# Expert stage of a routed transformer layer: the activated row is turned by VectorE in 32 by 32 blocks instead of by TensorE

## The chip, the cores and the metric

The kernel runs on one core of a Trainium2 chip. The metric is the device time of one execution in microseconds (us), the median of several runs. Every time of an instruction comes from one profiled execution.

## The reference, cut to what matters

The whole kernel computes an attention-like sampling layer, then a transformer block with multi-head attention and a mixture of experts, each followed by a layer norm. The change touches only the last part, the experts:

```python
logits = xf @ gate_w + gate_b
one_hot = jax.nn.one_hot(jnp.argmax(logits, axis=-1), E)
h = gelu(jnp.einsum('td,edh->teh', xf, w1), approximate=True)   # d = 256, h = 1024, E = 8
y = jnp.einsum('teh,ehd->ted', h, w2)
out = jnp.einsum('te,ted->td', one_hot, y)
...
x = _layernorm(x + L0_ffn(x), axis=-1)
```

There are 4096 tokens of 256 channels, in float32. Each token goes to one expert.

## The kernel before, in words

`build` runs its stages one after the other: wave parameters and sampling, gate and projection, attention, `project_and_route`, and last `experts` (L1742). The router has sorted the tokens by expert into a scratch tensor in memory, `routed`, in tiles of 128 tokens. No tile mixes experts, which makes MT = 39 tiles (L30). Two small tables, `tile_row` (named `at` in the code) and `expert`, say for each tile where its rows start and which expert it belongs to. The weights of all experts, `w1` and `w2`, lie in SBUF by then.

`experts` has one program for each engine, and semaphores order them. For tile j:

- SyncE (`load`, L1776) reads the row number from the table and loads the normalised row `z` (one buffer) and the residual row `res` (ring of 8).
- TensorE (`turn`, L1863) transposes z into PSUM `pZ`, and ScalarE (`norm`, L1815) applies the norm's weight and bias while it copies that to `zT`.
- TensorE's up projection (L1880) multiplies zT by w1 of the expert into `pH` (128 tokens by 1024 hidden values, two banks of PSUM). ScalarE's GELU (L1825) writes `hs` (`ex_h` in the profile), tokens on partitions.
- The down projection needs hidden values on partitions. So TensorE transposes the eight 128 by 128 squares of hs into PSUM `pT` (L1897), and VectorE copies all of pT to `hT` (L1853).
- TensorE's down projection (L1891) accumulates eight products of hT with w2 into `pY`, one expert row of 256 channels.
- VectorE adds the residual (L1842), takes mean and variance (L1844, L1848, with a one-element copy L1847 between them that makes the second wait for the first), and normalises (L1856), after GpSimd has computed 1/sqrt(variance + eps) (L1800, L1802). GpSimd then sends the row to its token's place in the output with an indirect DMA (L1805).

Order of work: each engine's program is written by hand, one tile deep. In iteration j TensorE does up(j), turn(j+1), down(j-1) and the transposes of hs(j). All tiles but the first and last two run in a hardware loop (`skewed`, L1761, with `Fori`). GpSimd's program is written out for all 39 tiles. `z`, `zT`, `hs`, `hT`, `pZ`, `pH`, `pT` and `pY` all have one buffer.

Of the kernel before, what the change touches and what calls it, by code (L numbers as in the profile page):

```python
# [18 lines left out]
KC = C // P  # L19
# [9 lines left out]
E, HID = 8, 1024  # L29
MT = TILES + E - 1  # L30
REGION = TOKENS + P
ROW = 2 * C + 4
# [22 lines left out]
def build(nc, io, dr):  # L55

    with ExitStack() as top:
# [39 lines left out]
        with ExitStack() as ctx:  # L97
            experts(nc, sem, lambda *a: sb(ctx, *a), lambda *a: ps(ctx, *a), io, dr, ident, w1, w2, expert, at)
# [1643 lines left out]
def experts(nc, sem, sb, ps, io, dr, ident, w1, w2, expert, at):  # L1742


    HC = HID // P
    ln_w, ln_b = sb("ex_lnw", [P, KC]), sb("ex_lnb", [P, KC])
    RES, OUTS = 8, 4
    z = sb("ex_z", [P, C])
    res = sb("ex_res", [P, RES, ROW - C])
    x, xo, st, mv, seen = sb("ex_x", [P, C]), sb("ex_out", [P, OUTS, C]), sb("ex_st", [P, 6]), sb("ex_mv", [P, 2]), sb("ex_seen", [P, 1])  # L1750
    eps, power, ve, rs = (sb("ex_" + n, [P, 1]) for n in ("eps", "power", "ve", "rs"))
    zT = sb("ex_zT", [P, KC, P])
    hs, hT = sb("ex_h", [P, HID]), sb("ex_hT", [P, HC, P])
    pZ, pH, pT, pY = ps("ex_pZ", [P, KC, P]), ps("ex_pH", [P, HID]), ps("ex_pT", [P, HC, P]), ps("ex_pY", [P, C])
    w_in, z_in, turned, zd, up, gelu, hturned, hTd, down, added = (sem("ex_" + n) for n in (
        "w_in", "z_in", "turned", "zT", "up", "gelu", "h_turned", "hT", "down", "added"))
    res_in, consts, stats, waited, aggred, inv, outd = (sem("ex_" + n) for n in ("res_in", "consts", "stats", "waited", "aggr", "rstd", "out"))
    sent = [sem(f"ex_sent{i}") for i in range(2)]
    out = io["out"].rearrange("b l c -> (b l) c")

    def skewed(eng, tile):  # L1761

        tile(0, None, True)
        tile(1, 0, True)
        with eng.Fori(2, MT - 1) as j:
            tile(j, j - 1, True)
        tile(MT - 1, MT - 2, False)
        tile(None, MT - 1, False)

    with nc.Block() as block, nc.allow_non_contiguous_dma(reason="per-channel vectors"):  # L1770
        @block.sync
        def _(sp):
            sp.dma_start(ln_w[:], io["L0_ffn_ln2_w"].rearrange("(k p) -> p k", p=P)).then_inc(w_in, 16)
            sp.dma_start(ln_b[:], io["L0_ffn_ln2_b"].rearrange("(k p) -> p k", p=P)).then_inc(w_in, 16)  # L1774

            def load(j):  # L1776
                row = sp.value_load(at[0:1, bass.ds(j, 1)], min_val=0, max_val=E * REGION - P)  # L1777
                if not isinstance(j, int) or j:

                    sp.wait_ge(turned, j)  # L1780
                sp.dma_start(z[:], dr["routed"][bass.ds(row, P), 0:C]).then_inc(z_in, 16)
                sp.dma_start(res[:, bass.ds(j % RES, 1), :].rearrange("p o c -> p (o c)"), dr["routed"][bass.ds(row, P), C:ROW]).then_inc(res_in, 16)

            load(0)
            with sp.Fori(1, MT) as j:
                load(j)

        @block.gpsimd
# [22 lines left out]
        @block.scalar  # L1811
        def _(a):
            a.wait_ge(w_in, 32)

            def norm(j):  # L1815
                a.wait_ge(turned, j + 1)
                a.wait_ge(up, j)
                for k in range(KC):
                    a.activation(zT[:, k, :], pZ[:, k, :], ACT.Identity, bias=ln_b[:, k:k + 1], scale=ln_w[:, k:k + 1]).then_inc(zd, 1)  # L1819

            def tile(j, prev, more):
                if j is not None:
                    a.wait_ge(up, j + 1)
                    a.wait_ge(hturned, j)
                    a.activation(hs[:], pH[:], ACT.Gelu_apprx_tanh).then_inc(gelu, 1)  # L1825
                if more:
                    norm(j + 1)

            norm(0)
            skewed(a, tile)  # L1830

        @block.vector
        def _(dve):
            v = nc.vector

            def tile(j, prev, more):
                if prev is not None:
                    dve.wait_ge(down, prev + 1)
                    dve.wait_ge(res_in, prev * 16 + 16)
                    if not isinstance(prev, int) or prev:  # L1840
                        dve.wait_ge(outd, prev)
                    v.tensor_tensor(x[:], pY[:], res[:, bass.ds(prev % RES, 1), 0:C].rearrange("p o c -> p (o c)"), ALU.add).then_inc(added, 1)  # L1842
                    dve.wait_ge(added, prev + 1)
                    v.bn_stats(st[:], x[:]).then_inc(stats, 1)  # L1844
                    dve.wait_ge(stats, prev + 1)

                    v.tensor_copy(seen[:], st[:, 0:1]).then_inc(waited, 1)  # L1847
                    v.bn_aggr(mv[:], st[:]).then_inc(aggred, 1)  # L1848
                if j is not None:
                    dve.wait_ge(hturned, j + 1)  # L1850
                    if prev is not None:
                        dve.wait_ge(down, j)
                    v.tensor_copy(hT[:], pT[:]).then_inc(hTd, 1)  # L1853
                if prev is not None:
                    dve.wait_ge(inv, prev * 2 + 2)
                    v.tensor_scalar(xo[:, bass.ds(prev % OUTS, 1), :].rearrange("p o c -> p (o c)"), x[:], mv[:, 0:1], rs[:],  # L1856
                                    ALU.subtract, ALU.mult).then_inc(outd, 1)

            skewed(dve, tile)

        @block.tensor
        def _(pe):
            def turn(j):  # L1863
                pe.wait_ge(z_in, j * 16 + 16)
                pe.wait_ge(zd, j * KC)
                for k in range(KC):
                    last = nc.tensor.transpose(pZ[:, k, :], z[:, k * P:(k + 1) * P], ident[:])  # L1867
                last.then_inc(turned, 1)

            def which(j):  # L1870
                return pe.value_load(expert[0:1, bass.ds(j, 1)], min_val=0, max_val=E - 1)

            def tile(j, prev, more):
                if j is not None:
                    e = which(j)
                    pe.wait_ge(zd, j * KC + KC)
                    pe.wait_ge(gelu, j)
                    for n in range(HID // 512):
                        for k in range(KC):
                            last = nc.tensor.matmul(pH[:, n * 512:(n + 1) * 512], zT[:, k, :],  # L1880
                                                    w1[:, k, bass.ds(e, 1), n * 512:(n + 1) * 512], start=(k == 0), stop=(k == KC - 1))
                    last.then_inc(up, 1)
                if more:
                    turn(j + 1)
                if prev is not None:
                    e = which(prev)
                    pe.wait_ge(hTd, prev + 1)
                    if j is None or not isinstance(j, int) or prev:
                        pe.wait_ge(added, prev)
                    for c in range(HC):  # L1890
                        last = nc.tensor.matmul(pY[:], hT[:, c, :], w2[:, c, bass.ds(e, 1), :], start=(c == 0), stop=(c == HC - 1))  # L1891
                    last.then_inc(down, 1)
                if j is not None:
                    pe.wait_ge(gelu, j + 1)
                    pe.wait_ge(hTd, j)
                    for c in range(HC):
                        last = nc.tensor.transpose(pT[:, c, :], hs[:, c * P:(c + 1) * P], ident[:])  # L1897
                    last.then_inc(hturned, 1)

            turn(0)  # L1900
            skewed(pe, tile)


SCRATCH = {
# [33 lines left out]
```

## Time and profile before

| what | value |
|---|---|
| median of 3 runs | 1881.21 us (1880.91 to 1882.89) |
| time of the profiled execution | 1883.31 us |
| its span, first to last instruction | 1881.1 us |
| expert stage, first SyncE instruction to the end of the span | 1550.09 to 1881.1 us |
| TensorE (PE) busy over the span | 86% |
| VectorE (DVE) busy over the span | 68% |

Engine names in rows: PE is TensorE's matrix unit, PEld its weight load, DVE VectorE, ACT ScalarE, POOL GpSimd, SP SyncE. Busy time counts an engine's running instructions; two that overlap in its pipeline count once in a stretch, so the mean duration of one instruction and the distance from one start to the next (the pitch below) can differ. Times are from the start of the span.

### The profile page before, as it was taken

The numbers are of one execution on the slowest core, as the hardware profiler recorded it, in microseconds if no ns is written. First come the engines' busy times: TensorE is split into PE (matmuls) and PEld (weight loads), VectorE is DVE, ScalarE is ACT, GpSimd is POOL, SyncE is SP. The second block draws the span as 40 slices with busy tenths as digits, with TensorE's granted clock in tenths as the row PEclk, the third lists the DMA queues.
The fourth block names the chain that finished last, engine by engine and source line by source line (L and its number), as shares of the span: only waits on it lengthen the run. The fifth ranks groups of instructions, "written<-read, shape, count | busy, mean of one in ns | idle before, by whom it ended". The sixth has DMA issues, their size and how long they took to land. (4 is left out here: it accounts for less than half of the span.)

```text
span 1881.1 us, 33148 instructions
## 1 busy us (share of the span) xinstructions
PE 1622.6 (86%) x9382; PEld 806.5 (43%) x9383; DVE 1273.7 (68%) x2358; ACT 1003.4 (53%) x1696; POOL 255.9 (14%) x426
## 2 busy tenths in 40 slices
PE   5049788878996899999999999999996829999997
PEld 5036555544553122322332332323225725777765
DVE  4889798754553888889888888888844742333333
ACT  3178797843444277767676777777772212222221
POOL 0011111102333000000000000000002661222222
PEclk9579999988998699999999999999998759999999
DMA  3010110113655532222222222223213531111110
GB/s 95 0 52 18 38 35 18 37 52 102 216 195 180 90 74 70 72 67 71 70 68 70 73 74 73 73 73 73 52 29 107 168 135 46 47 50 50 50 50 15
DMA packets 156230, 137.89 MB, mean 73 GB/s; under 512 B 73774, under 2 KB 129775, under 8 KB 156144
## 3 DMA queue, kind: packets, MB, share of 16 engines
q1 hardware_dynamic: 150096, 121.92, 23.5%
q0 software_dynamic: 5072, 14.77, 2.1%
q8 instruction: 31, 0.51, 0.1%
q14 instruction: 55, 0.45, 0.1%
q10 hardware_dynamic: 976, 0.24, 0.1%
HBM read 88.16 MB, written 49.23 MB: 73 GB/s over the span
## 5 line engine op out<-in xcount | busy, mean ns | idle before, releaser
L1253 DVE TENSOR_REDUCE at_mx<-at_pmx 128x1 f32<-128x512 f32 x1024 | 648.3, 682 | 75.8 <-PE at_pmx L1325 75.0
L1240 ACT ACTIVATE at_p<-at_pst 128x512 f32<-128x512 f32 x1024 | 540.0, 601 | 251.6 <-PE at_pst L1344 243.1
L1325 PE MATMUL at_pmx<-at_k,at_q 96*128 96x512 bf16 x1024 | 400.6, 393 | 16.9 <-DMA at_k<-scratch_ks 16.2
L1344 PE MATMUL at_pst<-at_q,at_k 99*128 99x512 bf16 x1024 | 352.2, 381 | 12.4 <-ACT at_p L1240 10.0
L1354 PE MATMUL at_pacc<-at_p,at_v 128*32 128x512 f32 x2048 | 272.7, 604 | 0.9 <-ACT at_p L1240 0.7
L1325 PEld LDWEIGHTS at_pmx<-at_k,at_q 96*128 96x128 bf16 x1024 | 99.7, 97 | 270.9 <-DVE at_mx L1253 196.2
L527 ACT ACTIVATE ws_A<-ws_steps,par_beta,par_alpha 128x672 f32<-128x672 bf16 (+2 forms) x256 | 200.4, 854 | 21.5 <-DVE ws_steps L603 16.0
L616 DVE TENSOR_TENSOR ws_AT<-ws_pA,ws_hitT 128x768 f32<-128x768 f32 (+1 forms) x192 | 180.5, 952 | 41.5 <-PE ws_pA L675 40.2
L675 PE MATMUL ws_pA<-ident,ws_A 128*128 128x128 f32 x1088 | 150.6, 285 | 26.0 <-ACT ws_A L527 21.2
L1344 PEld LDWEIGHTS at_pst<-at_q,at_k 99*128 99x128 bf16 x1024 | 99.3, 98 | 161.6 <-ACT at_p L1240 98.4
L1825 ACT ACTIVATE ex_h<-ex_pH 128x1024 f32<-128x1024 f32 x39 | 39.9, 1023 | 239.9 <-PE ex_pH L1880 239.9
L675 PEld LDWEIGHTS ws_pA<-ident,ws_A 128*128 128x128 f32 x1088 | 121.4, 145 | 84.8 <-DVE ws_AT L616 53.4
L1842 DVE TENSOR_TENSOR ex_x<-ex_pY,ex_res 128x256 f32<-128x256 f32 x39 | 16.5, 424 | 203.3 <-PE ex_pY L1891 203.3
L1880 PE MATMUL ex_pH<-w,ex_zT 128*128 x312 | 142.1, 599 | 1.0 <-ACT ex_zT L1819 1.0
L1891 PE MATMUL ex_pY<-w,ex_hT 128*128 x624 | 141.2, 379 | 1.6 <-DVE ex_hT L1853 1.6
L1891 PEld LDWEIGHTS ex_pY<-w,ex_hT 128*128 128x128 f32 x624 | 115.6, 190 | 16.4 <-issue 2.3
L1491 POOL MEMSET pg_eps<- 128x4 f32 x1 | 0.1, 106 | 803.5 <-POOLq L1121 803.5
L1880 PEld LDWEIGHTS ex_pH<-w,ex_zT 128*128 128x128 f32 x312 | 56.9, 192 | 58.4 <-issue 58.4
L1354 PEld LDWEIGHTS at_pacc<-at_p,at_v 128*32 128x32 f32 x2048 | 40.9, 107 | 94.4 <-ACT at_p L1240 61.5
L695 PE MATMUL ws_acc<-ws_AT,ws_x 128*32 128x384 f32 (+3 forms) x768 | 77.4, 480 | 0.0
L673 PE MATMUL ws_pA<-identb,ws_hit 128*128 128x128 bf16 x136 | 10.5, 232 | 73.9 <-DVE ws_steps L603 73.8
L1853 DVE COPY ex_hT<-ex_pT 128x1024 f32<-128x1024 f32 x39 | 47.7, 1223 | 27.7 <-PE ex_pT L1897 27.7
(237 smaller groups left out, 1659.1 us busy)
## 6 DMA issues: line engine op xcount, KB each, us to landing
w<-in_L_ffn_w SPq DMA_DIRECT2D x32, 512.0 KB, 4.8
at_q<-scratch_qs SPq DMA_DIRECT2D x192, 64.0 KB, 2.9
at_k<-scratch_ks SPq DMA_DIRECT2D x192, 64.0 KB, 3.0
scratch_v<-gp_v SPq DMA_DIRECT2D x8, 1024.0 KB, 5.6
at_v<-scratch_v SPq DMA_DIRECT2D x32, 256.0 KB, 3.5
scratch_qs<-gp_split SPq DMA_DIRECT2D x16, 384.0 KB, 2.6
scratch_ks<-gp_split SPq DMA_DIRECT2D x16, 384.0 KB, 3.4
ex_res<-scratch_routed SPq DMA_DIRECT2D x39, 130.0 KB, 2.3
```

The source lines that it names most:

```text
L527: nc.scalar.activation(A[:, h % QUAD, cols(g, r)], KB[g][:, cols(g, r)], ACT.Exp, bias=par["beta"][:, t, h], scale=par["alpha"][:, t, h]). ...
L616: v.tensor_tensor(AT[h // QUAD][:, home(h, m[0]):home(h, m[-1]) + 1, :].rearrange("p s l -> p (s l)"), p[:, 0:len(m) * P], mask, ALU.mult) ...
L675: last = nc.tensor.transpose(p[:, to], a, ident[:])
L695: last = nc.tensor.matmul(acc[hq][h4 * WD:(h4 + 1) * WD, rs[0] * P:(rs[-1] + 1) * P], xb[:, j, h * WD:(h + 1) * WD], AT[hq][:, home(h, s): ...
L1240: a.activation(pt[k // 2 % 4][:, k % 2, :], pst[bank(k)][:], ACT.Exp).then_inc(exped, 1)
L1253: v.reduce_max(mx[u % 2][:, m // 2, m % 2:m % 2 + 1], pmx[bank(m)][:], AX.X).then_inc(red, 1)
L1325: nc.tensor.matmul(pmx[bank(m)][:], qst[u][0:ROWS, h, nt * P:(nt + 1) * P], kst[u][0:ROWS, h, kh * HALF:(kh + 1) * HALF], start=True, stop ...
L1344: nc.tensor.matmul(pst[bank(k)][:], kst[u][:, h, t * P:(t + 1) * P], qst[u][:, h, p * HALF:(p + 1) * HALF], start=True, stop=True).then_in ...
L1354: last = nc.tensor.matmul(pacc[at:at + 2 * DK, :], vst[u][:, s, h, :], pt[(2 * s + p) % 4][:, h, :], start=(s == 0), stop=(s == BT - 1))
L1853: v.tensor_copy(hT[:], pT[:]).then_inc(hTd, 1)
L1880: last = nc.tensor.matmul(pH[:, n * 512:(n + 1) * 512], zT[:, k, :], w1[:, k, bass.ds(e, 1), n * 512:(n + 1) * 512], start=(k == 0), stop= ...
L1891: last = nc.tensor.matmul(pY[:], hT[:, c, :], w2[:, c, bass.ds(e, 1), :], start=(c == 0), stop=(c == HC - 1))
```

## The change

TensorE's eight transposes of hs and the PSUM tile pT go away, with VectorE's copy of 128 by 1024. In their place VectorE issues 16 transposes a tile. One takes 32 partitions of hs (quarter q), and of each of the eight 128-column squares the 32 columns of block b. It turns the eight 32 by 32 blocks so taken and writes them to the 32 partitions of quarter b of hT, in columns q*32 to q*32+32 of each square. So one such instruction has 256 elements on each of 32 partitions, source and destination in SBUF, both float32, and each of the 16 pairs (q, b) has one. VectorE's order for iteration j is: transposes with q = 0 and 1 of tile j, addition and statistics of tile j-2, transposes with q = 2 and 3 of tile j, normalisation of tile j-2. Nothing waits between the eight transposes of a half.

z, zT, hs, hT, pZ and pY get two buffers. pH keeps one. TensorE's iteration is up(j), turn(j+1), down(j-2). The loop over tiles is written out for all engines. SyncE loads tile 0's z ahead of the norm's weight and bias, and its loads wait for `turned` of one tile earlier than before. GpSimd's program is unchanged.

```diff
-    zT = sb("ex_zT", [P, KC, P])
-    hs, hT = sb("ex_h", [P, HID]), sb("ex_hT", [P, HC, P])
-    pZ, pH, pT, pY = ps("ex_pZ", [P, KC, P]), ps("ex_pH", [P, HID]), ps("ex_pT", [P, HC, P]), ps("ex_pY", [P, C])
+    zT = [sb(f"ex_zT{i}", [P, KC, P]) for i in range(2)]
+    hs, hT = ([sb(f"ex_{n}{i}", [P, HC, P]) for i in range(2)] for n in ("h", "hT"))
+    pZ = [ps(f"ex_pZ{i}", [P, KC, 2 * P]) for i in range(2)]
+    pH, pY = ps("ex_pH", [P, HID]), [ps(f"ex_pY{i}", [P, 2 * C]) for i in range(2)]
...
+            def load(j):
+                row = sp.value_load(at[0:1, j:j + 1], min_val=0, max_val=E * REGION - P)
+                if j >= 2:
+
+                    sp.wait_ge(turned, j - 1)
+                    sp.wait_ge(res_in[j % 2], j // 2 * 16)
+                sp.dma_start(z[j % 2][:], dr["routed"][bass.ds(row, P), 0:C]).then_inc(z_in[j % 2], 16)
+                if j >= RES:
+                    sp.wait_ge(sent[j % 2], (j - RES) // 2 * 16 + 16)
+                sp.dma_start(res[:, j % RES, :], dr["routed"][bass.ds(row, P), C:ROW]).then_inc(res_in[j % 2], 16)
+
...
+            norm(0)
+            for j in range(MT):
+                a.wait_ge(up, j + 1)
+                if j >= 2:
+                    a.wait_ge(hTd, j - 1)
+                a.activation(hs[j % 2][:].rearrange("p c n -> p (c n)"), pH[:], ACT.Gelu_apprx_tanh).then_inc(gelu, 1)
+                if j + 1 < MT:
                     norm(j + 1)
-
-            norm(0)
-            skewed(a, tile)
 
...
-                    v.tensor_copy(hT[:], pT[:]).then_inc(hTd, 1)
...
+            def turn_h(j, lanes):
+
+                u = j % 2
+                if 0 in lanes:
+                    dve.wait_ge(gelu, j + 1)
+                    if j >= 2:
+                        dve.wait_ge(down, j - 1)
+                for q in lanes:
+                    for b in range(P // Q):
+                        last = v.transpose(hT[u][b * Q:(b + 1) * Q, :, q * Q:(q + 1) * Q], hs[u][q * Q:(q + 1) * Q, :, b * Q:(b + 1) * Q])
+                if P // Q - 1 in lanes:
+                    last.then_inc(hTd, 1)
+
+            def add(j):
+                dve.wait_ge(down, j + 1)
+                dve.wait_ge(res_in[j % 2], j // 2 * 16 + 16)
+                if j:
+                    dve.wait_ge(outd, j)
+                v.tensor_tensor(x[:], pY[j % 2][:, 0:C], res[:, j % RES, 0:C], ALU.add).then_inc(added, 1)
+                dve.wait_ge(added, j + 1)
+                v.bn_stats(st[:], x[:]).then_inc(stats, 1)
+                dve.wait_ge(stats, j + 1)
+
+                v.tensor_copy(seen[:], st[:, 0:1]).then_inc(waited, 1)
+                if j:
+                    dve.wait_ge(inv, j * 2)
+                v.bn_aggr(mv[:], st[:]).then_inc(aggred, 1)
+
...
+            for j in range(MT + 2):
+                if j < MT:
+                    turn_h(j, range(0, 2))
+                if j >= 2:
+                    add(j - 2)
+                if j < MT:
+                    turn_h(j, range(2, 4))
+                if j >= 2:
+                    normalise(j - 2)
 
...
+            for j in range(MT + 2):
+                if j < MT:
                     e = which(j)
                     pe.wait_ge(zd, j * KC + KC)
-                    pe.wait_ge(gelu, j)
+                    if j:
+                        pe.wait_ge(gelu, j)
...
+                if j + 1 < MT:
                     turn(j + 1)
-                if prev is not None:
-                    e = which(prev)
-                    pe.wait_ge(hTd, prev + 1)
-                    if j is None or not isinstance(j, int) or prev:
-                        pe.wait_ge(added, prev)
+                if j >= 2:
+                    e = which(j - 2)
+                    pe.wait_ge(hTd, j - 1)
+                    if j >= 4:
+                        pe.wait_ge(added, j - 3)
                     for c in range(HC):
-                        last = nc.tensor.matmul(pY[:], hT[:, c, :], w2[:, c, bass.ds(e, 1), :], start=(c == 0), stop=(c == HC - 1))
+                        last = nc.tensor.matmul(pY[j % 2][:, 0:C], hT[j % 2][:, c, :], w2[:, c, bass.ds(e, 1), :], start=(c == 0), stop=(c == HC - 1))
                     last.then_inc(down, 1)
-                if j is not None:
-                    pe.wait_ge(gelu, j + 1)
-                    pe.wait_ge(hTd, j)
-                    for c in range(HC):
-                        last = nc.tensor.transpose(pT[:, c, :], hs[:, c * P:(c + 1) * P], ident[:])
```

## Rows read from the trace of the kernel before

**Rows 1.** Busy time in one stretch of the stage; columns as in the header.

```profile
core 0: us, PE busy (x) PEld busy (x) DVE busy (x) ACT busy (x) POOL busy (x), PEclk, DMA share, GB/s
1625.00:1665.00 40.00, 40.00 (x172) 27.85 (x172) 13.29 (x30) 8.60 (x15) 8.87 (x15) 1.00 0.16 49
```

**Rows 2.** Chain of waits, one period: start us, us, what.

```profile
1643.32 3.44 PE ex_pH L1880 x8
1646.76 0.22 PE ex_pZ L1867 x2
1646.98 3.46 PE ex_pY L1891 x16
1650.43 0.87 PE ex_pT L1897 x8
1651.31 3.44 PE ex_pH L1880 x8
```

**Rows 3.** Groups by line in the expert stage: busy us, mean ns | idle before, releaser.

```profile
L1853 DVE COPY ex_hT<-ex_pT 128x1024 f32<-128x1024 f32 x39 | 47.7, 1223 | 27.7 <-PE ex_pT L1897 27.7
...
L1825 ACT ACTIVATE ex_h<-ex_pH 128x1024 f32<-128x1024 f32 x39 | 39.9, 1023 | 239.9 <-PE ex_pH L1880 239.9
...
L1842 DVE TENSOR_TENSOR ex_x<-ex_pY,ex_res 128x256 f32<-128x256 f32 x39 | 16.5, 424 | 203.3 <-PE ex_pY L1891 203.3
```

**Rows 4.** Timeline of VectorE, one tile: start us, us.

```profile
1650.81 0.42 DVE L1842 TENSOR_TENSOR ex_x<-ex_pY,ex_res 128x256 f32<-128x256 f32 x1 [5.24 <-PE ex_pY L1891]
1651.27 0.43 DVE L1844 BATCH_NORM_STATS2 ex_st<-ex_x 128x6 f32<-128x256 f32 x1
1651.73 0.15 DVE L1847 COPY ex_seen<-ex_st 128x1 f32<-128x1 f32 x1
1651.81 0.17 DVE L1848 BATCH_NORM_AGGREGATE ex_mv<-ex_st 128x2 f32<-128x6 f32 x1
1651.90 1.22 DVE L1853 COPY ex_hT<-ex_pT 128x1024 f32<-128x1024 f32 x1
1653.14 0.41 DVE L1856 TENSOR_SCALAR ex_out<-ex_x,ex_mv,ex_rs 128x256 f32 x1
```

**Rows 5.** Timeline of VectorE in the routing stage, four operations without a wait.

```profile
1509.54 1.41 DVE L1622 BATCH_NORM_STATS2 pg_st<-pg_x 128x6 f32<-128x256 f32 x4
```

**Rows 6.** Groups of VectorE by shape, whole span.

```profile
L1622 DVE BATCH_NORM_STATS2 pg_st<-pg_x 128x6 f32<-128x256 f32 x32 | 11.2, 414 | 0.3
...
L1667 DVE TENSOR_TENSOR pg_past<-pg_js,pg_cum 1x312 f32<-1x312 f32 x1 | 0.5, 472 | 0.0
```

**Rows 7.** Chain of waits, start and end of the stage.

```profile
1550.09 0.38 SPq L1773
1550.52 0.46 SPq L1774
...
1561.27 1.03 ACT ex_h L1825
1562.35 1.09 PE ex_pT L1897 x8
...
1868.08 0.13 issue
1868.21 2.01 PE ex_pY L1891 x9
```

**Rows 8.** Timeline of the last tile, with the idle time before it.

```profile
1868.21 3.72 PE L1891 MATMUL ex_pY<-w,ex_hT 128*128 x16 [1.58 <-DVE ex_hT L1853]
...
1875.36 1.03 POOL L1805 DMA_INDIRECT out<-ex_out,ex_res  x1 [1.26 <-DVE ex_out L1856]
```

**Rows 9.** Timeline of the routing stage: VectorE beside GpSimd.

```profile
1513.39 3.42 DVE L1633 TENSOR_SCALAR pg_n<-pg_x,pg_mv,pg_rs 128x256 f32<-128x256 f32 x4 [1.98 <-POOL pg_rs L1525]
1513.95 2.39 POOL L1530 TENSOR_TENSOR pg_rows<-pg_x,pg_y 128x1024 f32<-128x1024 f32 x1 [0.59 <-DMA scratch_routed<-pg_rows,pg_slot]
```

**Rows 10.** Busy time and granted clock in three stretches.

```profile
1554.00:1559.00 5.00, 3.77 (x6) 1.81 (x7) 0.00 (x0) 2.09 (x3) 0.00 (x0) 0.50 0.23 63
...
1515.00:1530.00 15.00, 6.59 (x52) 5.96 (x52) 7.39 (x34) 2.38 (x3) 10.07 (x14) 0.50 0.37 142
1868.20:1871.90 3.70, 3.69 (x16) 2.96 (x16) 0.19 (x1) 0.00 (x0) 1.02 (x1) 1.00 0.01 0
```

More of the change, by code:

```diff
@@ L1745, in experts @@
     HC = HID // P
+    Q = 32
     ln_w, ln_b = sb("ex_lnw", [P, KC]), sb("ex_lnb", [P, KC])
     RES, OUTS = 8, 4
-    z = sb("ex_z", [P, C])
+    z = [sb(f"ex_z{i}", [P, C]) for i in range(2)]
     res = sb("ex_res", [P, RES, ROW - C])
@@ L1751, in experts @@
     eps, power, ve, rs = (sb("ex_" + n, [P, 1]) for n in ("eps", "power", "ve", "rs"))
-    zT = sb("ex_zT", [P, KC, P])
-    hs, hT = sb("ex_h", [P, HID]), sb("ex_hT", [P, HC, P])
-    pZ, pH, pT, pY = ps("ex_pZ", [P, KC, P]), ps("ex_pH", [P, HID]), ps("ex_pT", [P, HC, P]), ps("ex_pY", [P, C])
-    w_in, z_in, turned, zd, up, gelu, hturned, hTd, down, added = (sem("ex_" + n) for n in (
-        "w_in", "z_in", "turned", "zT", "up", "gelu", "h_turned", "hT", "down", "added"))
-    res_in, consts, stats, waited, aggred, inv, outd = (sem("ex_" + n) for n in ("res_in", "consts", "stats", "waited", "aggr", "rstd", "out"))
+    zT = [sb(f"ex_zT{i}", [P, KC, P]) for i in range(2)]
+    hs, hT = ([sb(f"ex_{n}{i}", [P, HC, P]) for i in range(2)] for n in ("h", "hT"))
+    pZ = [ps(f"ex_pZ{i}", [P, KC, 2 * P]) for i in range(2)]
+    pH, pY = ps("ex_pH", [P, HID]), [ps(f"ex_pY{i}", [P, 2 * C]) for i in range(2)]
+    w_in, turned, zd, up, gelu, hTd, down, added = (sem("ex_" + n) for n in (
+        "w_in", "turned", "zT", "up", "gelu", "hT", "down", "added"))
+    z_in = [sem(f"ex_z_in{i}") for i in range(2)]
+    res_in = [sem(f"ex_res_in{i}") for i in range(2)]
+    consts, stats, waited, aggred, inv, outd = (sem("ex_" + n) for n in ("consts", "stats", "waited", "aggr", "rstd", "out"))
     sent = [sem(f"ex_sent{i}") for i in range(2)]
     out = io["out"].rearrange("b l c -> (b l) c")
[L1761 to L1768, printed above, removed]
     with nc.Block() as block, nc.allow_non_contiguous_dma(reason="per-channel vectors"):
@@ L1772, in _ @@
         def _(sp):
+            def load(j):
[7 more added lines that the diff above has]
+                sp.dma_start(res[:, j % RES, :], dr["routed"][bass.ds(row, P), C:ROW]).then_inc(res_in[j % 2], 16)
+            load(0)
             sp.dma_start(ln_w[:], io["L0_ffn_ln2_w"].rearrange("(k p) -> p k", p=P)).then_inc(w_in, 16)
             sp.dma_start(ln_b[:], io["L0_ffn_ln2_b"].rearrange("(k p) -> p k", p=P)).then_inc(w_in, 16)
[L1776 to L1785, printed above, removed]
+            for j in range(1, MT):
                 load(j)
@@ L1816, in norm @@
                 a.wait_ge(turned, j + 1)
-                a.wait_ge(up, j)
+                if j >= 2:
+                    a.wait_ge(up, j - 1)
                 for k in range(KC):
-                    a.activation(zT[:, k, :], pZ[:, k, :], ACT.Identity, bias=ln_b[:, k:k + 1], scale=ln_w[:, k:k + 1]).then_inc(zd, 1)
-            def tile(j, prev, more):
-                if j is not None:
[L1823 to L1826, printed above, removed]
+                    a.activation(zT[j % 2][:, k, :], pZ[j % 2][:, k, 0:P], ACT.Identity, bias=ln_b[:, k:k + 1],
+                                 scale=ln_w[:, k:k + 1]).then_inc(zd, 1)
+            norm(0)
[5 more added lines that the diff above has]
+                if j + 1 < MT:
                     norm(j + 1)
-            norm(0)
-            skewed(a, tile)
         @block.vector
@@ L1834, in _ @@
             v = nc.vector
-            def tile(j, prev, more):
-                if prev is not None:
[L1838 to L1852, printed above, removed]
-                    v.tensor_copy(hT[:], pT[:]).then_inc(hTd, 1)
[L1854 to L1857, printed above, removed]
@@ L1859, in _ @@
-            skewed(dve, tile)
+            def turn_h(j, lanes):
[9 more added lines that the diff above has]
+                    last.then_inc(hTd, 1)
@@ new lines, in normalise @@
+            def normalise(j):
+                dve.wait_ge(inv, j * 2 + 2)
+                if j >= OUTS:
+                    dve.wait_ge(sent[j % 2], (j - OUTS) // 2 * 16 + 16)
+                v.tensor_scalar(xo[:, j % OUTS, :], x[:], mv[:, 0:1], rs[:], ALU.subtract, ALU.mult).then_inc(outd, 1)
+            for j in range(MT + 2):
[7 more added lines that the diff above has]
+                    normalise(j - 2)
@@ L1863, in turn @@
             def turn(j):
-                pe.wait_ge(z_in, j * 16 + 16)
-                pe.wait_ge(zd, j * KC)
+                pe.wait_ge(z_in[j % 2], j // 2 * 16 + 16)
+                if j >= 2:
+                    pe.wait_ge(zd, (j - 1) * KC)
                 for k in range(KC):
-                    last = nc.tensor.transpose(pZ[:, k, :], z[:, k * P:(k + 1) * P], ident[:])
+                    last = nc.tensor.transpose(pZ[j % 2][:, k, 0:P], z[j % 2][:, k * P:(k + 1) * P], ident[:])
                 last.then_inc(turned, 1)
@@ L1870, in which @@
             def which(j):
-                return pe.value_load(expert[0:1, bass.ds(j, 1)], min_val=0, max_val=E - 1)
-            def tile(j, prev, more):
-                if j is not None:
+                return pe.value_load(expert[0:1, j:j + 1], min_val=0, max_val=E - 1)
+            turn(0)
+            for j in range(MT + 2):
+                if j < MT:
                     e = which(j)
                     pe.wait_ge(zd, j * KC + KC)
-                    pe.wait_ge(gelu, j)
+                    if j:
+                        pe.wait_ge(gelu, j)
@@ L1878, in tile @@
                     for n in range(HID // 512):
                         for k in range(KC):
-                            last = nc.tensor.matmul(pH[:, n * 512:(n + 1) * 512], zT[:, k, :],
+                            last = nc.tensor.matmul(pH[:, n * 512:(n + 1) * 512], zT[j % 2][:, k, :],
                                                     w1[:, k, bass.ds(e, 1), n * 512:(n + 1) * 512], start=(k == 0), stop=(k == KC - 1))
                     last.then_inc(up, 1)
-                if more:
+                if j + 1 < MT:
@@ L1884, in tile @@
                     turn(j + 1)
-                if prev is not None:
-                    e = which(prev)
-                    pe.wait_ge(hTd, prev + 1)
-                    if j is None or not isinstance(j, int) or prev:
-                        pe.wait_ge(added, prev)
+                if j >= 2:
+                    e = which(j - 2)
+                    pe.wait_ge(hTd, j - 1)
+                    if j >= 4:
+                        pe.wait_ge(added, j - 3)
                     for c in range(HC):
-                        last = nc.tensor.matmul(pY[:], hT[:, c, :], w2[:, c, bass.ds(e, 1), :], start=(c == 0), stop=(c == HC - 1))
+                        last = nc.tensor.matmul(pY[j % 2][:, 0:C], hT[j % 2][:, c, :], w2[:, c, bass.ds(e, 1), :], start=(c == 0), stop=(c == HC - 1))
@@ L1892, in tile @@
                     last.then_inc(down, 1)
-                if j is not None:
-                    pe.wait_ge(gelu, j + 1)
-                    pe.wait_ge(hTd, j)
-                    for c in range(HC):
-                        last = nc.tensor.transpose(pT[:, c, :], hs[:, c * P:(c + 1) * P], ident[:])
-                    last.then_inc(hturned, 1)
-            turn(0)
-            skewed(pe, tile)
 SCRATCH = {
```

## The prediction

> **What bounds the kernel now.** I read the stage by windows first: between 1625 and 1665 us TensorE is busy for all of 40.00 us at a granted clock of 1.00, and VectorE for 13.29 us [rows 1]. So TensorE sets the pace here, and VectorE is two thirds idle. The chain of waits says the same in detail: one tile is up projection 3.44, turning z 0.22, down projection 3.46, turning the activated row 0.87 us, 7.99 in all, one behind the other with no wait between [rows 2]. The other engines wait for TensorE: in the groups by line VectorE's addition stands behind 203.3 us of idle time that TensorE ended, ScalarE's GELU behind 239.9 us [rows 3]. The sum of the four parts is the period, so the hardware loop costs nothing now and writing it out can give nothing.
>
> **The part that goes.** TensorE loses 0.87 us a tile, which lies wholly on the path [rows 2]: 39 x 0.87 = 34 us is the most that the change can bring. TensorE's tile becomes 3.44 + 0.22 + 3.46 = 7.12 us. VectorE loses the copy of 128 by 1024, 1.22 us [rows 4], which was beside TensorE's work and is worth nothing by itself.
>
> **The part that comes.** VectorE gets 16 transpositions a tile, of 256 elements in each of 32 partitions. That only 32 partitions take part doesn't make one cheap: an operation on a single partition with 312 elements took 472 ns, one on 128 partitions with 256 elements 414 ns [rows 6]. What counts is the number of elements a partition, and so the 16 cost 16 operations of 256 elements. No row shows a transposition on VectorE. The pitch from one to the next is bounded by two patterns. Four operations of 128 by 256 with no wait between, all on the same partitions, took 1.41 us together [rows 5] at 0.41 each [rows 6]: (1.41 - 0.41) / 3 = 0.33 us pitch, since each begins while the one before is still running. Where one waits for the other's result, the pitch is 0.46 us: 1650.81 to 1651.27, and again to 1651.73 [rows 4].
>
> I take 0.46. Each of the 16 writes another quarter of the partitions than the one before, and the overlap was only seen where nothing moves, so I count none. Around it: with no overlap and no gap either it would be the duration alone, 0.42. Upwards, a block of 32 columns must be in before its first turned column can come out. By rows 4 an element costs (1.22 - 0.42) / 768 = 1.04 ns, so filling costs 33 ns, and emptying as much again: 0.46 + 0.067 = 0.53.
>
> A rule of the Trainium skill speaks against this change as well: the page "VectorE: DVE Perf Modes", section "Two Vector instructions with no wait between them", says that an instruction whose input or output starts in another group of 32 partitions than that of the last one starts only when every earlier one has finished. All 16 would be held by it. No trace here shows it, since all operations of VectorE before start at partition 0. By the rule the pitch is a full duration; without it the time would be that of the first rival.
>
> VectorE's other work for a tile: from the addition's start to the end of the statistics 1650.81 to 1651.98, 1.17 us; the normalisation 0.41 and a gap of 0.04 [rows 4]. Together 1.62. VectorE's tile is then 16 x 0.46 + 1.62 = **8.98 us, against TensorE's 7.12**. VectorE becomes the bound, and TensorE waits 1.9 us a tile for hT.
>
> **The sum.** VectorE starts on tile 0 when its GELU is done, at 1562.35 [rows 7]. From then it runs without a break: 39 x 7.36 = 287.0 for transpositions, 37 x 1.62 = 59.9 for the tiles finished between them, less 0.45 because the last normalisation stands behind the last transposition. With 0.13 us from hT to TensorE [rows 7] the last down projection starts at 1562.35 + 287.0 + 59.9 - 0.45 + 0.13 = 1909.0, where it was 1868.21 [rows 7, 8]. What follows it stays the same: 3.72 us of products, addition, statistics, normalisation, the last transfer [rows 8]. That is +40.8 us on a span of 1881.1: 1921.9, or 1924.1 for the profiled execution's 1883.3. The median shown is 2.1 us below that execution, so I forecast **1922 us**.
>
> **Edits with no price, and what covers them.** The waits added to VectorE's path: ahead of the first transposition of tile j it waits for down(j-2), which TensorE can start as soon as tile j-2 is turned, nearly a whole period earlier, and which takes 3.46 of 8.98 us. The wait for GpSimd's root (1651.98 to 1653.14, 1.16 us [rows 4]) now has eight transpositions in front, 3.7 us. ScalarE's GELU(j) now waits until tile j-2 is turned, with norm(j+1) queued behind it and so up(j+1). It is released 0.45 us before VectorE takes up tile j-1, and its 1.02 us [rows 3] are needed one tile later. With a period of 7.12 these covers would still hold: a down projection ends 3.66 us before the next one begins. z's load is one tile earlier, with a second buffer; it didn't stand in the chain of the steady tiles. SyncE issues z ahead of two small loads of 0.38 and 0.46 us [rows 7], worth 0.8 us at most once, and nothing where ScalarE then waits for those two; I take nothing.
>
> **Price of being wrong on the pitch.** 624 transpositions make 6.24 us for each 0.01 us. The change breaks even where 40.8 us are saved: 0.46 - 0.065 = 0.395 us.
>
> **Rivals.**
> First, on the other side: the 16 overlap like those of rows 5. Pitch 0.33, VectorE 16 x 0.333 + 1.62 = 6.95 us a tile, below 7.12. TensorE stays the bound. It does up(1) and turn(2) until 1566.0, then 37 tiles of 7.12 until 1829.5; VectorE turns tile 38 with an addition and statistics in between (5.33 + 1.17, + 0.13), and the last down projection starts at 1836.1: -32.1, **1849 us**. For it: no semaphore stands between the 16 and none reads what another writes, as in rows 5. Against it: they change partitions at each step. It decides at a pitch below 0.395. Chance 0.13.
>
> Second, VectorE is blocked by GpSimd. In the routing stage four operations from SBUF to SBUF took 3.42 us beside a GpSimd operation of 2.39 us, where 1.41 is the undisturbed time [rows 5, 9]. GpSimd is busy for 8.87 us in 40, 1.77 a tile [rows 1]. If all of it blocked transpositions: 37 x 1.77 = +65, 1987 us. Against it: addition, statistics and normalisation run clear of GpSimd now, and only one of the kinds of operation, the normalising one, shows the effect. Beside it stands a transposition that moves an element in two steps: pitch 0.46 + 0.27 = 0.73, +168, 2090 us. Also TensorE's clock: it was 0.50, its lower level of 1.2 GHz, where TensorE had stood idle for long before or was busy for 6.59 of 15 us, but 1.00 after a wait of 1.58 us before the last down projection [rows 8, 10]. Here it is busy for 7.12 of 8.98 with pauses of 1.9 us; I count on 1.00, and the slack of 1.9 us would take up part of a fall. Together 0.06.
>
> Third, the pitch comes out within 0.006 of 0.395, and gain and loss cancel: 1881 us. Chance 0.01.
>
> **Numbers.** The forecast, VectorE the bound at a pitch of 0.41 to 0.53, has 0.80. Its ends are 1922 - 31 = 1891 and 1922 + 42 = 1964 us, and as it holds 8 in 10 alone, the range is its own: 1890 to 1964. Faster by over 0.2% (about what a measurement of this kernel can tell from no change) is the first rival, 0.13; within 0.2% 0.02, the third rival and the edge of the forecast beside it; slower the rest, 0.85.
>
> **What would show it.** Right: VectorE busy for nearly all of each tile; period 8.6 to 9.9 us; the last of its waits before TensorE's down projection, about 1.9 us a tile; starts of the transpositions one full duration apart, and the 4 within the same input quarter no closer than those across two; ScalarE and GpSimd as before. Wrong: TensorE still busy throughout and a period of 7.12 (first rival); transpositions longer where GpSimd is at work, or one with a duration of over 0.6 us (second); a granted clock below 1.00 in the steady tiles.

## The result and the profile after

The changed kernel takes **1912.87 us** (median of 4 runs, 1912.18 to 1917.05), the kernel before beside it 1881.86 us (4 runs). The ratio is 1.0169, 95% interval 1.0157 to 1.0182: slower by 1.7%, 31 us. The profiled execution took 1912.18 us, with a span of 1910.5 us. Forecast were 1922 us and a range of 1890 to 1964.

The page of the changed kernel: span, busy time of TensorE, and the chain that ended last by engine and by line (L1842 is the new transposition).

```profile
span 1910.5 us, 32366 instructions
PE 1599.3 (84%) x9070; PEld 775.1 (41%) x9070; DVE 1497.4 (78%) x2943; ACT 1003.3 (53%) x1696; POOL 256.5 (13%) x426
...
DVE 15%; issue 3%; PE 1%; POOL 0%; DMA 0%; SPq 0%; ACT 0%; POOLq 0%
DVE ex_hT L1842 12%; DVE ex_st L1853 1%; DVE ex_x L1851 1%; DVE ex_out L1865 1%; PE ex_pH L1899 0%; DVE ex_seen L1856 0%; PE ex_pY L1910 0%; DVE ex_mv L1859 0%; DMA ex_lnb<-in_L_ffn_ln_b 0%; POOL out L1802 0%; ACT ex_h L1825 0%; ACT ex_zT L1817 0%; SPq L1769 0%; POOL ex_rs L1799 0%; SPq L1780 0%
```

Of the whole span 15% is now VectorE's chain in this stage. In the kernel before the same line of the page had TensorE there:

```profile
PE 17%; issue 0%; DVE 0%; DMA 0%; POOL 0%; SPq 0%; ACT 0%; POOLq 0%; ACTq 0%
```

Busy time in a stretch of the stage, with the header of the columns, answers to [rows 1]:

```profile
core 0: us, PE busy (x) PEld busy (x) DVE busy (x) ACT busy (x) POOL busy (x), PEclk, DMA share, GB/s
1660.00:1700.00 40.00, 33.17 (x122) 22.24 (x122) 38.49 (x96) 8.60 (x15) 8.12 (x13) 1.00 0.18 50
```

VectorE is busy for 38.5 of 40 us (before 13.3), and TensorE only for 33.2 of 40 (before 40.0). TensorE's clock stayed at 1.00 through its short pauses. The groups by line answer to [rows 3]:

```profile
L1842 DVE STREAM_TRANSPOSE ex_hT<-ex_h 32x256 f32<-32x256 f32 x624 | 271.8, 436 | 37.0 <-ACT ex_h L1825 28.2
...
L1802 POOL DMA_INDIRECT out<-ex_out,ex_res x39 | 40.1, 1027 | 147.3 <-DVE ex_out L1865 143.1 <-issue 4.2
L1825 ACT ACTIVATE ex_h<-ex_pH 128x1024 f32<-128x1024 f32 x39 | 39.9, 1023 | 260.8 <-DVE ex_hT L1842 237.0 <-PE ex_pH L1899 23.8
...
L1851 DVE TENSOR_TENSOR ex_x<-ex_pY,ex_res 128x256 f32<-128x256 f32 x39 | 16.6, 425 | 0.9 <-PE ex_pY L1910 0.3
```

The 624 transpositions take 436 ns each. The waits have turned round: the addition, which stood behind 203.3 us of TensorE's work, now waits for 0.9 us in all, and GELU's idle time is ended by VectorE (237.0 us) and only for 23.8 us by TensorE. The timeline of VectorE for one tile answers to [rows 4] (start us, us):

```profile
1700.20 0.42 DVE L1851 TENSOR_TENSOR ex_x<-ex_pY,ex_res 128x256 f32<-128x256 f32 x1
1700.66 0.43 DVE L1853 BATCH_NORM_STATS2 ex_st<-ex_x 128x6 f32<-128x256 f32 x1
1701.12 0.15 DVE L1856 COPY ex_seen<-ex_st 128x1 f32<-128x1 f32 x1
1701.19 0.17 DVE L1859 BATCH_NORM_AGGREGATE ex_mv<-ex_st 128x2 f32<-128x6 f32 x1
1701.39 3.59 DVE L1842 STREAM_TRANSPOSE ex_hT<-ex_h 32x256 f32<-32x256 f32 x8
1705.02 0.41 DVE L1865 TENSOR_SCALAR ex_out<-ex_x,ex_mv,ex_rs 128x256 f32<-128x256 f32 x1
1705.35 3.57 DVE L1842 STREAM_TRANSPOSE ex_hT<-ex_h 32x256 f32<-32x256 f32 x8
1708.93 0.42 DVE L1851 TENSOR_TENSOR ex_x<-ex_pY,ex_res 128x256 f32<-128x256 f32 x1
```

One period runs from 1700.20 to 1708.93, 8.73 us. Eight transpositions run from 1701.39 to the start of the normalisation at 1705.02, eight more from 1705.35 to the next addition at 1708.93. TensorE over the same stretch:

```profile
1703.38 0.38 PE L1884 MATMUL ex_pZ<-ident,ex_z 128*128 128x128 f32 x2
1705.12 3.72 PE L1910 MATMUL ex_pY<-w,ex_hT 128*128 x16 [1.36 <-DVE ex_hT L1842]
```

It has z turned, behind the up projection, at 1703.8 and waits 1.36 us for hT, until 1705.12. That is the wait that took the place of the old bound.

### The profile page after: what moved, and what is told of

Its sections match the earlier page's. It is cut to its first block and busy times, and to the rows that moved or that the text cites. A ratio compares the mean times of both kernels' runs of the same rounds, so it can differ in the third digit from the quotient of the medians.

```text
span 1910.5 us, 32366 instructions
## 1 busy us (share of the span) xinstructions
PE 1599.3 (84%) x9070; PEld 775.1 (41%) x9070; DVE 1497.4 (78%) x2943; ACT 1003.3 (53%) x1696; POOL 256.5 (13%) x426
## 5 line engine op out<-in xcount | busy, mean ns | idle before, releaser
L1842 DVE STREAM_TRANSPOSE ex_hT<-ex_h 32x256 f32<-32x256 f32 x624 | 271.8, 436 | 37.0 <-ACT ex_h L1825 28.2
L1910 PE MATMUL ex_pY<-w,ex_hT 128*128 x624 | 146.5, 388 | 53.5 <-DVE ex_hT L1842 53.4
L1825 ACT ACTIVATE ex_h<-ex_pH 128x1024 f32<-128x1024 f32 x39 | 39.9, 1023 | 260.8 <-DVE ex_hT L1842 237.0
L1020 PE MATMUL gp_pQ<-gp_zT,gp_wqkv 128*128 128x512 f32 x128 | 60.1, 607 | 1.5 <-ACT gp_zT L869 1.5
```

Source lines behind the costliest of these rows:

```text
L1842: last = v.transpose(hT[u][b * Q:(b + 1) * Q, :, q * Q:(q + 1) * Q], hs[u][q * Q:(q + 1) * Q, :, b * Q:(b + 1) * Q])
L1910: last = nc.tensor.matmul(pY[j % 2][:, 0:C], hT[j % 2][:, c, :], w2[:, c, bass.ds(e, 1), :], start=(c == 0), stop=(c == HC - 1))
```

## The experiments

Every run is compared with runs of the kernel before on the same chip. The edits are shown shortened, as differences from the changed kernel. The medians of the kernel before were 1884.55 us beside the first four kernels, 1882.20 beside the first run of each of the last two experiments, and 1882.53 beside the second. One thing has to be kept apart: in the profiles the expert stage begins anywhere between 1546.9 and 1553.1 us, though the stages ahead of it have the same code in all. So mechanisms are read from periods within the stage, and differences of totals of 2 or 3 us are not argued from.

### Same partitions

```diff
-  last = v.transpose(hT[u][b * Q:(b + 1) * Q, :, q * Q:(q + 1) * Q], hs[u][q * Q:(q + 1) * Q, :, b * Q:(b + 1) * Q])
+  last = v.transpose(hT[u][:, q, :, b * Q:(b + 1) * Q], hs[u][:, :, b * Q:(b + 1) * Q])   # hT four times as large
...
```

The kernel leaves out most of the turning: each block of 32 by 32 is turned within its own quarter, and the down projection reads one of the four parts of hT.

Expected:

> Leaves out part of the computation: each of the 16 transpositions a tile takes all 128 partitions from partition 0 and turns blocks within their own quarter only, so the row isn't fully turned; count and elements (256 a partition) are those of the changed kernel. Theory 1 (a transposition waits for the end of the one before because it starts in other partitions): here nothing moves, the pitch falls from 0.448 to 0.33 to 0.35 us as for the four statistics of rows 5, VectorE's tile to 6.9 to 7.2 us, TensorE is the bound again at 7.12 and the time is 1849 to 1856 us. Rival (a transposition never overlaps with the next, whatever its partitions): pitch 0.45, period 8.73, the time stays at 1913 us.

Measured: 1854.96 us, ratio 0.9848 (0.9832 to 0.9865). One period in the timeline:

```profile
1650.20 3.62 PE L1910 MATMUL ex_pY<-w,ex_hT 128*128 x16
1650.51 2.70 DVE L1842 STREAM_TRANSPOSE ex_hT<-ex_h 128x256 f32<-128x256 f32 x8
1653.92 2.73 DVE L1842 STREAM_TRANSPOSE ex_hT<-ex_h 128x256 f32<-128x256 f32 x8 [0.42 <-PE ex_pY L1910]
1657.31 3.62 PE L1910 MATMUL ex_pY<-w,ex_hT 128*128 x16
```

Eight transpositions take 2.70 us instead of 3.59. With 0.40 us for the last, the pitch is (2.70 - 0.40) / 7 = 0.33 us, that of the four statistics of [rows 5]. The period is that of TensorE's down projection, 1650.20 to 1657.31, 7.11 us, and VectorE now waits before each tile for it. The rival, that transpositions never overlap, is out. The run also shows the rest of the first rival of the prediction to be sound: with a pitch of 0.33 the change would have brought about 30 us, as its sum said.

### Four patterns

```diff
+  ins = outs = slice(0, P)
+  if j >= 9:
+      o, i = ((0, 0), (b, 0), (0, b))[(j - 9) // 10]
+      outs, ins = slice(o * Q, (o + 1) * Q), slice(i * Q, (i + 1) * Q)
-  last = v.transpose(hT[u][b * Q:(b + 1) * Q, :, q * Q:(q + 1) * Q], hs[u][q * Q:(q + 1) * Q, :, b * Q:(b + 1) * Q])
+  last = v.transpose(hT[u][outs, q, :, b * Q:(b + 1) * Q], hs[u][ins, :, b * Q:(b + 1) * Q])
...
```

This kernel leaves out part of the turning as well. The order is: 128 partitions; first quarter to first; first quarter to a changing one; a changing quarter to the first.

Expected:

> Leaves out part of the computation as its transpositions turn only some of the blocks; it is run for its pitches. 16 transpositions of 256 elements a tile: tiles 0 to 8 on all 128 partitions, 9 to 18 from the first quarter to the first, 19 to 28 from the first quarter to a changing one, 29 to 38 from a changing quarter to the first. Theory 1: pitch 0.33 to 0.35 in the first two groups, 0.45 in the last two, so a period of about 7.1 and then 8.7 us. If only the written quarter counts, the last group is at 0.33 to 0.35 too; if only the read one, the third is. Rival (transpositions never overlap): 0.45 in all four. If 32 partitions are cheaper than 128 in themselves, the second group is below the first.

Measured: one run, 1882.63 us. One half tile of each pattern, in the order of the expectation:

```profile
1579.69 2.69 DVE L1846 STREAM_TRANSPOSE ex_hT<-ex_h 128x256 f32<-128x256 f32 x8
...
1643.64 2.69 DVE L1846 STREAM_TRANSPOSE ex_hT<-ex_h 32x256 f32<-32x256 f32 x8
...
1718.64 3.54 DVE L1846 STREAM_TRANSPOSE ex_hT<-ex_h 32x256 f32<-32x256 f32 x8
...
1804.25 3.53 DVE L1846 STREAM_TRANSPOSE ex_hT<-ex_h 32x256 f32<-32x256 f32 x8
```

And the busy time of a stretch in the second and in the fourth (length, PE, PEld, DVE, ACT, POOL, clock, DMA):

```profile
1645.00:1680.00 35.00, 35.00 (x130) 23.17 (x129) 32.42 (x105) 8.08 (x15) 8.65 (x15) 1.00 0.19 57
1800.00:1835.00 35.00, 30.31 (x110) 19.77 (x109) 33.73 (x87) 7.73 (x15) 7.45 (x13) 1.00 0.15 42
```

Eight transpositions take 2.69, 2.69, 3.54 and 3.53 us: a pitch of 0.33 without a change of partitions, on 128 or on 32 of them, and of 0.44 as soon as either side changes, the written one or the read one. It is a property of the step from one instruction to the next. It also shows that 32 partitions are no cheaper than 128, as [rows 6] had suggested. In the stretch without a change TensorE is busy for all 35 us, in the one with a change for 30.3. By the Trainium skill, page "VectorE: DVE Perf Modes", section "Two Vector instructions with no wait between them", a change of the starting group of 32 partitions on either side holds an instruction until all earlier ones are finished; this trace agrees, for each side alone.

### The buffers alone

```diff
-  turn_h(j, range(0, 2)); add(j - 2); turn_h(j, range(2, 4))
+  add(j - 2); copy_h(j)              # VectorE: PSUM pT to hT, 128 by 1024
...
+  for c in range(HC):                # TensorE, behind down(j-2)
+      last = nc.tensor.transpose(pT[:, c, :], hs[j % 2][:, c, :], ident[:])
```

Expected:

> TensorE's transposes and VectorE's copy from PSUM are put back, everything else of the change stays (two buffers, down projection two tiles behind, loop written out). My account gives these edits no price: period 7.99 us as before, 1881 us within 0.3%. Rival: they cost or give something of their own that the change's 31 us contain, for instance 3 us that the stages ahead of the experts gained in the changed kernel's profile; then the time differs from 1881 by that.

Measured: 1882.63 us (10 runs), ratio 0.9991 (0.9979 to 1.0002): no difference. The chain of waits over one period:

```profile
1700.05 3.43 PE ex_pH L1892 x8
1703.48 0.22 PE ex_pZ L1877 x2
1703.70 3.46 PE ex_pY L1903 x16
1707.16 0.87 PE ex_pT L1910 x8
1708.03 3.44 PE ex_pH L1892 x8
```

The parts are those of [rows 2] to 0.01 us, 7.98 in sum. Second buffers, the later down projection and the written out loop together cost nothing and give nothing that the interval would show (at most 0.2%, 4 us). So the 31 us belong to the transpositions.

### Two tiles in one transposition

```diff
-  last = v.transpose(hT[u][b * Q:(b + 1) * Q, :, q * Q:(q + 1) * Q], hs[u][q * Q:(q + 1) * Q, :, b * Q:(b + 1) * Q])
+  last = v.transpose(hT[u][b * Q:(b + 1) * Q, 0:n, :, q * Q:(q + 1) * Q].rearrange("p t c n -> p (t c) n"),
+                     hs[u][q * Q:(q + 1) * Q, 0:n, :, b * Q:(b + 1) * Q].rearrange("p t c n -> p (t c) n"))   # n = 2 tiles
...
-  if j >= 2:                         # TensorE
+  if j >= 4:                         # down(j - 4)
```

VectorE's order changes with it: one addition with its statistics stands ahead of the first four transpositions of a pair, the other ahead of the last twelve.

Expected:

> The same blocks are turned, but for two tiles at once: 16 transpositions of 512 elements for each pair of tiles, down projection four tiles behind. If a held transposition costs a fixed 0.18 us plus 1.04 ns an element, the pitch is 0.715 us, VectorE needs 16 x 0.715 + 2 x 1.62 = 14.7 us a pair, 7.34 a tile, against TensorE's 7.12: the time is about 1863 us, below both kernels. Rival (the time is in the elements, nothing fixed to save): pitch 0.9, VectorE 8.8 us a tile, 1913 us or a little more for the longer end.

Measured: 1873.33 us, ratio 0.9939 (0.9923 to 0.9956): faster than both kernels, though 10 us over the expectation. From the timeline:

```profile
1703.45 8.58 DVE L1839 STREAM_TRANSPOSE ex_hT<-ex_h 32x512 f32<-32x512 f32 x12
...
1713.70 2.81 DVE L1839 STREAM_TRANSPOSE ex_hT<-ex_h 32x512 f32<-32x512 f32 x4
...
1718.27 8.59 DVE L1839 STREAM_TRANSPOSE ex_hT<-ex_h 32x512 f32<-32x512 f32 x12
```

Twelve transpositions of 512 elements take 8.58 us: (8.58 - 0.70) / 11 = 0.716 us, as expected, against 2 x 0.448 = 0.896 for two of 256. So about 0.18 us of each held transposition is fixed and only the rest goes with its elements. The period of a pair is 14.82 us (1703.45 to 1718.27), 7.41 a tile, where 7.34 was expected. That explains 3 of the 10 us. The rest lies outside the steady period. VectorE begins at 1568.64 us, when GELU has done tile 1, and tile 0 was done 5.6 us before that, at 1563.01. Behind the last transposition (1855.94) 16.5 us follow to the end of the span, where it is 13.4 us in the changed kernel (1897.12). How much of these 8.7 us the expected 1863 already held is open.

### Four squares on each engine

```diff
-  last = v.transpose(hT[u][b * Q:(b + 1) * Q, :, q * Q:(q + 1) * Q], hs[u][q * Q:(q + 1) * Q, :, b * Q:(b + 1) * Q])
+  v.transpose(hT[u][b * Q:(b + 1) * Q, 0:4, q * Q:(q + 1) * Q], hs[u][q * Q:(q + 1) * Q, 0:4, b * Q:(b + 1) * Q])
+  nc.tensor.transpose(pT[:, c - 4, :], hs[j % 2][:, c, :], ident[:])      # c = 4 to 7, TensorE
+  v.tensor_copy(hT[j % 2][:, 4:, :], pT[:]).then_inc(hTd, 1)
```

Expected:

> Of each tile's eight squares VectorE turns four (16 transpositions of 128 elements a partition) and TensorE the other four, which VectorE copies from PSUM. Held transpositions at 0.448 us for 256 elements and 1.04 ns an element less make 0.315 us each: VectorE 5.04 + 0.68 for the copy + 1.62 = 7.3 us a tile, TensorE 7.12 + 4 x 0.109 = 7.55 and the bound: 39 x 0.43 us less than before, 1866 us. If instead a held transposition has a floor near 0.40 us, VectorE needs 8.7 us and the time is 1910 us.

Measured: 1876.78 us (10 runs), ratio 0.9975 (0.9963 to 0.9986): faster than before by 0.25%, less than expected. The price of a transposition was right: 16 of 128 elements take 2.52 us for each eight, with 0.30 us for the last a pitch of 0.317 us, where 0.315 was expected. VectorE was not in the way, it waits 0.2 to 0.5 us a tile for TensorE. TensorE's down projections in the timeline come alternately 7.92 and 7.56 us apart:

```profile
1656.61 3.62 PE L1915 MATMUL ex_pY<-w,ex_hT 128*128 x16
...
1664.53 3.62 PE L1915 MATMUL ex_pY<-w,ex_hT 128*128 x16
...
1672.09 3.62 PE L1915 MATMUL ex_pY<-w,ex_hT 128*128 x16
```

In every second tile there is a pause in the weight loads, ahead of the up projection, with no releaser:

```profile
1707.14 0.30 PEld L1904 LDWEIGHTS ex_pH<-w,ex_zT 128*128 128x128 f32 x2 [0.33 <-issue]
```

The second run of the pair tests one cause for it: TensorE reads the number of the tile's expert (`which`) just there.

```diff
+  if j + 1 < MT:
+      up_e = which(j + 1)            # the table's read, ahead of the four transposes
   pe.wait_ge(gelu, j + 1)
...
-  e = which(j)
+  e = up_e
```

Expected:

> As split4, but TensorE reads the next tile's expert number from the table ahead of its four transposes and not behind them. In split4 the period was about 7.8 us and not 7.55, with TensorE's weight load idle 0.33 us ahead of each up projection with no releaser shown. If that is the table's read, which only 0.44 us of transposes cover there (0.87 in the kernel before), the period falls to 7.55 us and the time to about 1866 us. If it is something else (TensorE slower beside VectorE's transpositions), the time stays at 1876 us.

Measured: 1869.90 us, ratio 0.9926 (0.9909 to 0.9942). The chain of waits:

```profile
1703.68 3.46 PE ex_pY L1916 x16
1707.14 0.44 PE ex_pT L1925 x4
1707.58 3.44 PE ex_pH L1905 x8
1711.01 0.22 PE ex_pZ L1889 x2
1711.23 3.46 PE ex_pY L1916 x16
```

3.46 + 0.44 + 3.44 + 0.22: the period is 7.55 us for every tile (1703.68 to 1711.23), and the idle time is gone. So it was the read of the expert's number from SBUF into a register: 0.87 us of transposes in front of it cover it in the kernel before, and 0.44 us here do not in every tile. The time is 4 us above the expected 1866, though the period is the expected one. In this profile the stage began 3.0 us later than in that of the kernel before (1553.1 and 1550.1); how the rest divides was not worked out.

### No transposition at all

```diff
-  nc.tensor.matmul(pH[:, n * 512:(n + 1) * 512], zT[j % 2][:, k, :], w1[:, k, bass.ds(e, 1), n * 512:(n + 1) * 512], start=(k == 0), stop=(k == KC - 1))
+  nc.tensor.matmul(pH[:, c, :], wst[j % 2][:, k, c * P:(c + 1) * P], zT[j % 2][:, k, :], start=(k == 0), stop=(k == KC - 1))
+  v.tensor_copy(wst[j % 2][:], w1[:, :, bass.ds(e, 1), :].rearrange("p k o n -> p (k o) n"))        # VectorE
-  a.activation(hs[j % 2][:].rearrange("p c n -> p (c n)"), pH[:], ACT.Gelu_apprx_tanh)
+  a.activation(hT[j % 2][:], pH[:], ACT.Gelu_apprx_tanh)
```

The product is the same, with its two sides exchanged: the weights stand still and the 128 tokens move, so the result has hidden values on partitions as it leaves TensorE. VectorE first copies the expert's weights to a fixed place (`wst`, two buffers), so that the stationary side's address doesn't depend on the expert.

Expected:

> No transposition of the activated row at all: the up projection takes the weights as its stationary side and gives 128 hidden values by 128 tokens at once, so GELU writes hT itself. VectorE copies the expert's 2048 weights a partition to a fixed place for it, 1.1 to 2.2 us a tile beside 1.62 of its own. TensorE's tile is up projection of 32 pairs of weight load and product, turning z 0.22, down projection 3.46. If weight loads hide behind the products as in the transposes (pitch 0.109 us), the up projection takes 3.5 us, the tile 7.2 and the time is about 1850 us; if each pair takes its weight load's 0.19 us, it takes 6.1, the tile 9.8 and the time is about 1950 us.

Measured: 2088.85 us, ratio 1.1095 (1.1077 to 1.1114), far worse than either end of the expectation. From the timeline and the windows:

```profile
1707.87 0.42 DVE L1840 TENSOR_TENSOR ex_x<-ex_pY,ex_res 128x256 f32<-128x256 f32 x1 [9.23 <-PE ex_pY L1903]
...
1710.82 1.23 DVE L1860 COPY ex_w<-w 128x2048 f32 x1 [0.36 <-issue]
...
1712.10 4.20 PE L1892 MATMUL ex_pH<-ex_zT,ex_w 128*128 128x128 f32 x21 [4.26 <-DVE ex_w L1860]
```

```profile
1700.00:1740.00 40.00, 27.24 (x149) 24.95 (x149) 8.20 (x18) 5.16 (x9) 7.26 (x9) 0.84 0.10 30
```

The expectation had priced the engines and missed the order on VectorE: the copy for tile j+2 stood behind the addition of tile j, which waits for down(j), which TensorE does just before up(j+2). So TensorE waited 4.26 us a tile for the copy, and its granted clock was 0.84 over the stretch, where it had been 1.00 in the kernel before. The next run moves the copy ahead of the addition, and nothing else.

```diff
+  if j + 2 < MT:
+      pick(j + 2)
   add(j)
   normalise(j)
-  if j + 2 < MT:
-      pick(j + 2)
```

Expected:

> As up_turned, but VectorE copies the next weights ahead of its addition and not behind it. There TensorE waited 4.3 us a tile for the copy, because the addition before it waits for the down projection. Without that wait TensorE is the bound: 32 pairs at 0.167 us (26 took 4.44 us) make 5.3 us, the tile 9.0 and the time about 1922 us; at the 0.13 us of the transposes' weight loads it would be 7.9 and 1878 us.

Measured: **1851.06 us**, ratio 0.9835 (0.9818 to 0.9851): 1.65% faster than the kernel before, 31 us, with nothing of the computation left out. The chain of waits:

```profile
1702.26 3.46 PE ex_pY L1903 x16
1705.71 3.57 PE ex_pH L1892 x32
1709.28 0.22 PE ex_pZ L1877 x2
1709.50 3.46 PE ex_pY L1903 x16
```

The 32 pairs take 3.57 us, 0.112 us each. That is below both prices expected, which had been taken from a stretch with a lowered clock (0.167) and from a weight load's length in the transposes (0.13). The period is 7.24 us (1702.26 to 1709.50): all of the 0.87 us of the transposes is saved for 0.13 us more of up projection. The time is that of the better end of the expectation for the run before, 1850 us, which had the pitch of 0.109 us.

## Why the prediction was right, point by point

**The bound moves to VectorE: right, and shown.** The windows, the exchange of the waits and the period of 8.73 us say so. TensorE's 7.12 us of work leave 1.61 us of that period (1.36 by the wait in the timeline), where 1.9 were forecast for the longer period of 8.98. The range held the time, and the mechanism is the one of the forecast. The rival with its time of 1849 us needed a pitch of 0.33, and at that pitch the chip gave 1854.96 us.

**No overlap where the partitions change: right, and shown** by the four patterns. In the prediction this was a choice between two rows with no row to decide it; the argument given ("only seen where nothing moves") turned out to be the right one. Had it been the other way, the sign of the result would have been wrong.

**The pitch of 0.46: a little high.** Eight take 3.58 to 3.63 us with the step to the next operation, 0.448 to 0.454 each, within an input quarter as across two. The forecast had put together 0.42 of duration and 0.04 of gap, from a pair with a semaphore between; the held ones have 0.436 of duration and a gap of 0.01. That the two errors nearly cancel is luck. Of 16 x 0.46 = 7.36 us a tile, 3.58 + 3.63 = 7.21 were used, and 39 x 0.15 = 5.9 us of the forecast were too much. The upper bound, with 0.067 us for filling and emptying a block, was not needed: in place of it a transposition lasts 436 ns where a sum of the same size lasts 425.

**VectorE's other work of 1.62: too much by 0.1.** It is 1700.20 to 1701.39 and 1705.02 to 1705.35, 1.19 + 0.33 = 1.52 us. The transposition behind the normalisation starts while that still runs, since both read and write from partition 0: the rule at work in the other direction. So it holds 15 of the 16 and not all, as the prediction had it. 37 x 0.1 are 3.7 us.

**The sum.** From the first transposition to the last down projection the forecast had 1909.0 - 1562.35 = 346.7 us, and the trace has 1559.92 to 1897.26, 337.3. The two terms above, 5.9 and 3.7, explain the difference of 9.4. The stage began 3.2 us earlier in this profile, of which the first tile gave back some: its up projection took 6.36 us for 5.32. So VectorE began 2.4 us earlier, and 0.3 us more followed behind the start of the last down projection; the span of 1910.5 is 11.4 us below the forecast 1921.9. Neither is a part of the mechanism. The median missed by only 9 us because the forecast took off 2.1 us from the profiled execution, and here the median lies 0.7 us above it. That this is again the size of the two terms is chance.

**Edits with no price: right.** The run with the buffers alone shows it for the buffers, the order and the written out loop. For the added waits the changed kernel's timeline shows it: between 1700.20 and 1708.93 VectorE waits for nothing, so GELU, GpSimd's root and the loads stayed covered.

**Blocking by GpSimd: not there.** Between 1600 and 1800 us the transpositions last 426 to 441 ns, with GpSimd at work beside some of them and not beside others. GpSimd's pieces there are short, 0.18, 0.57 and 1.03 us; whether an operation like that of [rows 9], 2.39 us on 128 by 1024, would hold up a transposition is not shown.

**The clock: right where it mattered.** In the steady tiles the granted clock stayed at 1.00 with pauses of 1.4 us. Only near the end, where no up projection is left to fill the time, did it fall:

```profile
1888.53 5.60 PE L1910 MATMUL ex_pY<-w,ex_hT 128*128 x16 [5.02 <-DVE ex_hT L1842]
...
1897.26 3.71 PE L1910 MATMUL ex_pY<-w,ex_hT 128*128 x16 [3.13 <-DVE ex_hT L1842]
```

The last down projection but one took 5.60 us after a pause of 5.02, with a granted clock of 0.50 in its first 2 us, and nothing waited for it.

## What to carry to other kernels

Work moved from a full engine to an idle one must fit in the idle one's time, counted as starts one behind the other and not as busy time of an average. Sixteen short transpositions that step through the partitions cost their full duration each, so make them few and long, or share them between both engines. Better still, ask whether the product before can deliver the layout that is wanted: exchanging its two sides removed the transposition for a copy of the weights on VectorE, and beat every way of turning the whole row that was tried. The order of the work on the engine that gets the copy decided between 11% slower and 1.65% faster.

## What the runs showed that I had not expected

VectorE pays for a change of quarter on either side alone, 0.45 us a piece against 0.33. The overlap lost is only a part of it. One without a change lasts 0.403 us, and the next begins 0.08 us before its end; one with a change lasts 0.436 us, and 0.01 us pass before the next.

A read of a table into a register of TensorE's program costs up to 0.36 us where the work in front of it is short (0.44 us), and nothing where it is 0.87 us.

Exchanging the sides of a float32 product of 128 by 256 by 1024 cost TensorE only 3.57 us for 3.44, although it loads weights 32 times instead of 8. In that kernel GpSimd was disturbed by VectorE's plain copy from SBUF to SBUF, 128 by 2048:

```profile
L1804 POOL DMA_INDIRECT out<-ex_out,ex_res x39 | 63.2, 1620 | 49.4 <-DVE ex_out L1854 47.8 <-issue 1.6
```

GpSimd's indirect DMA lasts 1620 ns on average there, where it lasts 1027 beside the transpositions. The last three of the 39, which have no copy beside them, last 1024 to 1030 ns. So the copy holds GpSimd up, and the transpositions don't.
